# One slot table for both lots in the second expert layer, and one lookup for both choices

## The reference, cut to what matters

```python
x = x + _L0_attn_ref(_layernorm(x), ...)   # linear recurrence and a small MLP
x = x + _L0_ffn_ref(_layernorm(x), ...)    # 8 experts, 128 -> 256 -> 128, best 2 per row
x = x + _L1_attn_ref(_layernorm(x), ...)   # causal attention, 16 heads of 8
x = x + _L1_ffn_ref(_layernorm(x), ...)    # 8 experts, 128 -> 512 -> 128, best 2 per row
```

```python
scores = jax.nn.sigmoid(xf @ gate_w + bias)
top_scores, top_idx = jax.lax.top_k(scores, K)                  # K = 2 of E = 8
top_scores = top_scores / (jnp.sum(top_scores, axis=-1, keepdims=True) + 1e-06)
up = jnp.einsum('th,ehi->tei', xf, up_w) + up_b
eo = jnp.einsum('tei,eih->teh', gelu(up), down_w) + down_b      # only the 2 chosen are needed
combined = jnp.einsum('teh,te->th', eo * 0.1, w)
shared = (gelu(xf @ sw_up + sb_up) @ sw_down + sb_down) * 0.1
out = (shared + combined) / (max |shared + combined| per row + 1e-06)
```

## Time and profile before

| | |
|---|---|
| three executions | 942.72, 943.45, 945.0 us |
| the profiled execution, its own time | 942.91 us |
| its span (first to last instruction) | 941.1 us |
| PE busy | 792.7 us (84%), 5585 instructions |
| DVE busy | 603.0 us (64%) |
| ACT busy | 530.5 us (56%) |
| POOL busy | 425.1 us (45%) |
| mean granted TensorE clock | 0.925 of full |

### The profile page before, as it was taken

How to read it: one execution, slowest core, us unless ns; L and a number is a source line. 1 busy time by engine, 2 the same in 40 slices (tenths; PEclk the granted TensorE clock), 3 DMA queues, 4 the chain that set the end, 5 groups by cost and what they waited for, 6 DMA issues and landing times. The chain is left out here.

```text
span 941.1 us, 18633 instructions
## 1 busy us (share of the span) xinstructions
PE 792.7 (84%) x5585; PEld 596.8 (63%) x5585; DVE 603.0 (64%) x1378; ACT 530.5 (56%) x1108; POOL 425.1 (45%) x527
## 2 busy tenths in 40 slices
PE   2798833899749899999999999996648999999993
PEld 2566633898625556565655566554626999999773
DVE  5478744557649887777777777752650565678455
ACT  3466457566416566767677676674322656655541
POOL 2655467727468414232323332223367730372274
PEclk9999775999879999999999999997569999999997
DMA  5940013546253231313131312100012332342222
GB/s 142 367 125 1 17 48 95 176 124 164 70 176 124 65 99 37 101 33 100 34 105 41 105 53 82 34 1 1 9 42 78 113 105 59 98 115 64 80 70 64
DMA packets 82155, 80.45 MB, mean 85 GB/s; under 512 B 9856, under 2 KB 61758, under 8 KB 82110
## 3 DMA queue, kind: packets, MB, share of 16 engines
q1 hardware_dynamic: 73122, 62.68, 21.8%
q0 software_dynamic: 8192, 16.79, 6.1%
q10 hardware_dynamic: 796, 0.42, 0.2%
HBM read 41.06 MB, written 38.80 MB: 85 GB/s over the span
## 5 line engine op out<-in xcount | busy, mean ns | idle before, releaser
L1678 ACT ACTIVATE Pb<-ps,low 128x512 f32<-128x512 f32 x320 | 216.7, 689 | 131.4 <-PE ps L1777 87.5
L935 POOL DMA_INDIRECT YG<-yslots,slot x128 | 131.0, 1024 | 134.9 <-issue 69.9
L1556 DVE TENSOR_REDUCE m<-ps 128x4 f32<-128x1024 f32 x128 | 156.0, 1220 | 53.4 <-PE ps L1754 35.6
L1777 PE MATMUL ps<-Q,KZ 128*128 128x128 f32 (+3 forms) x512 | 172.1, 397 | 5.0 <-ACT Pb L1678 4.0
L392 POOL DMA_INDIRECT xslots<-XN,slot x128 | 125.7, 982 | 69.6 <-issue 37.6
L1487 POOL TENSOR_SCALAR_AFFINE_SELECT Pb<-Pb 128x512 f32<-128x512 f32 (+1 forms) x84 | 67.6, 805 | 190.1 <-ACT Pb L1678 189.4
L1777 PEld LDWEIGHTS ps<-Q,KZ 128*128 128x128 f32 x512 | 93.0, 192 | 81.8 <-ACT Pb L1678 56.1
L1341 PE MATMUL ps<-wdn,hb 128*128 128x128 f32 x960 | 133.9, 276 | 6.1 <-ACT hb L1160 5.7
L1163 ACT ACTIVATE hb<-ps,upb 128x128 f32<-128x128 f32 x320 | 91.4, 369 | 66.6 <-PE ps L1329 66.6
L1754 PE MATMUL ps<-KZ,Q 128*128 128x512 f32 x320 | 113.6, 433 | 13.9 <-DMA KZ<-terms 8.8
L1341 PEld LDWEIGHTS ps<-wdn,hb 128*128 128x128 f32 x960 | 120.1, 193 | 7.6 <-DVE yb L1193 6.9
(11 more groups left out here) (262 smaller groups left out, 1275.5 us busy)
## 6 DMA issues: line engine op xcount, KB each, us to landing
xt<-xslots SPq DMA_DIRECT2D x40, 256.0 KB
yslots<-yb SPq DMA_DIRECT2D x40, 256.0 KB, 2.3
terms<-high SPq DMA_DIRECT2D x32, 256.0 KB, 2.2
Q<-terms SPq DMA_DIRECT2D x128, 48.0 KB
KZ<-terms SPq DMA_DIRECT2D x128, 48.0 KB
xslots<-YG SPq DMA_DIRECT2D x2, 2560.0 KB, 11.8
terms<-low SPq DMA_DIRECT2D x16, 256.0 KB, 2.3
X<-in_L_attn_x_dram SPq DMA_DIRECT2D x4, 512.0 KB, 5.9
```

What stands on the lines that cost most here:

```text
L935: pool.indirect_dma_start(out=s.YG[:, TB * w + j, k, :], out_offset=None, in_=s.yslots[group][:, :], in_offset=bass.IndirectOffsetOnAxis(a ...
L1556: w = dve.tensor_reduce(top[:, :, (TB + 1, 3, TB, None, 1)[u]], ps.rearrange("p (t g k) -> p g t k", t=2, g=HG), AX.XY, ALU.max)
L1678: act.activation(Pb[:, NCH * (gg % 2) + c, :], bank(4 + c % 2), ACT.Exp, bias=s.low[:, :], scale=DH ** -0.5)\
L1777: w = pe.matmul(ps[:, col:col + T - kt * P], KZ[:, HG * gg + g, kt * P:kt * P + P], Q2[gg % 2][:, kt * P:T], start=True, stop=not masked)
```

## The change

In the second layer the two tables of 40 tiles become one of 72 (2 x 32 tiles of rows and 8 part tiles), so 9 bodies. The table is ordered by what the first lot fills: first the tiles that the first lot fills wholly, then the tiles that it begins and the second lot goes on with, then the tiles that only the second lot uses. At least 25 tiles are of the first sort, so the first 24 (`WHOLE`), three bodies, can be worked before the second lot is in; from body 3 on SP waits for the second lot's scatters. The first lot's rows lie in the first 40 tiles (`TOUCHED`), so its gathers wait for 5 bodies, as before. The first layer keeps its two lots of 40 tiles.

The second layer's places come from a new function, `place_phases`. In both functions the two choices are now looked up in one operation, the slots are announced (`placed`) before the tiles' expert numbers are worked out, and the matrix that counts rows before gives the count less one table (`before` filled with 0 and -1), so that one subtraction falls away. Both layers use one DRAM array for the table. The core of the diff:

```diff
-SLOTS = sum(GS)
-BODIES = SLOTS // (2 * TB)
+BT = 2 * TB
+WHOLE = (2 * TB * GROUPS[0] - (E - 1)) // BT * BT
+TOUCHED = -(-(2 * TB * GROUPS[0] + E - 1) // BT) * BT
+SLOTS = (sum(GS), -(-(2 * TB * B + E - 1) // BT) * BT)
+TILES = max(SLOTS)
...
@@ place (first layer)
     link(dve.tensor_tensor_scan(flatC, keep, inside, 0.0, ALU.mult, ALU.add))
-    link(dve.tensor_copy(tot, C[:, :, count - 1]))
-    link(dve.tensor_tensor(flatC, flatC, inside, ALU.subtract))
-    link(dve.tensor_tensor(flatC, flatC, before, ALU.add))
-    link(dve.tensor_scalar(toti, tot, float(P - 1), None, ALU.add))
+    link(dve.tensor_scalar(toti, C[:, :, count - 1], float(P - 1), None, ALU.add))
+    link(dve.tensor_tensor(flatC, flatC, behind, ALU.add))
...
+    hot = s.hot[:, :, tiles, :]
+    link(dve.tensor_tensor(hot, hot, place_of, ALU.mult))
+    link(dve.tensor_reduce(s.pos[:, :, tiles], hot, AX.X, ALU.add))
+    link(dve.tensor_scalar(s.slot[:, :, tiles], s.pos[:, :, tiles], 0.0, None, ALU.add))
+    dve.nop().then_inc(s.placed, 1)
...
-    for k in range(2):
-        hot, gt = s.hot[:, k, tiles, :], s.gt[:, tiles]
-        link(dve.tensor_tensor(hot, hot, pos, ALU.mult))
-        link(dve.tensor_reduce(gt, hot, AX.X, ALU.add))
-        if k == 0:
-            link(dve.tensor_copy(s.slot[:, k, tiles], gt))
-        else:
-            dve.tensor_copy(s.slot[:, k, tiles], gt).then_inc(s.placed, 1)
+    dve.nop().then_inc(s.numbered, 1)
...
+def place_phases(dve, s, link, g):
...
+    if g == 1:
+        heads = inside.rearrange("p (e j) -> p e j", e=E)[:, :, 0]
+        link(dve.tensor_tensor(heads, heads, s.count[:, :], ALU.add))
+    link(dve.tensor_tensor_scan(flatC, keep, inside, 0.0, ALU.mult, ALU.add))
+    total = C[:, :, count - 1]
+    if g == 0:
+        dve.tensor_copy(s.count[:, :], total)
+        dve.tensor_scalar(s.tilesi[:, 0, :], total, 0.0, None, ALU.add)
+    link(dve.tensor_scalar(s.tilesi[:, 1, :], total, float(P - 1), None, ALU.add))
+    link(dve.tensor_tensor(flatC, flatC, behind, ALU.add))
+    if g == 0:
+        link(dve.tensor_scalar(s.tilesi[:, :, :], s.tilesi[:, :, :], 7, None, ALU.arith_shift_right))
+        link(dve.tensor_copy(s.tiles[:, 0:4:3, :], s.tilesi[:, :, :]))
+        link(dve.tensor_tensor(part, begun, whole, ALU.subtract))
+        link(dve.tensor_tensor_scan(flat(s.tends, 0, 2), ones(2), flat(s.tiles, 0, 2), 0.0, ALU.mult, ALU.add))
+        link(dve.tensor_tensor(s.shifts[:, 0:2, :], s.tends[:, 0:2, :], s.tiles[:, 0:4:3, :], ALU.subtract))
+    else:
...
+    limit, low, step = (whole, begun)[g], s.shifts[:, g, :], s.step[:, g, :]
+    link(dve.tensor_tensor(step, s.shifts[:, g + 1, :], low, ALU.subtract))
+    link(dve.scalar_tensor_tensor(over, bc(limit), float(P), C, ALU.mult, ALU.is_le))
+    link(dve.tensor_tensor(over, over, bc(step), ALU.mult))
+    link(dve.tensor_tensor(over, over, bc(low), ALU.add))
+    link(dve.scalar_tensor_tensor(C, over, float(P), C, ALU.mult, ALU.add))
...
+    here, classes = slice((0, WHOLE)[g], (WHOLE, SLOTS[1])[g]), (1, 3)[g]
+    wide = [1, here.stop - here.start, classes * E]
...
+    link(dve.tensor_tensor(cmp, s.tileno[0:1, here].unsqueeze(2).broadcast_to(wide),
+                           flat(s.tends, 0, classes)[0:1, :].unsqueeze(1).broadcast_to(wide), ALU.is_ge))
+    link(dve.tensor_reduce(s.tef[0:1, here], cmp, AX.X, ALU.add))
...
@@ experts
+    BODIES = SLOTS[layer] // BT
+    SECOND, LAST = (SLOT0[1], WHOLE)[layer] // BT, [n // BT for n in (TOUCHED, SLOTS[layer])]
...
             rows_in(0)
-            for r in two:
-                load(0, 0, r)
-            for g in range(NG):
-
+            for n in range(2):
                 for r in two:
-                    load(g, 1, r)
-                    if g > 0:
-                        store(g - 1, GB[g - 1] - 1, r)
-                with sp.Fori(1, GB[g] - 1) as n:
+                    load(n, r)
+            for g, (start, end) in enumerate(((2, SECOND), (SECOND, BODIES))):
+                if g > 0:
+                    rows_in(g)
+                with sp.Fori(start, end) as n:
                     for r in two:
-                        load(g, n + 1, r)
-                        store(g, n - 1, r)
...
+                        load(n, r)
+                        store(n - 2, r)
...
-                    pool.wait_ge(stored[r], 16 * (BODY0[g] + GB[g]))
+                    pool.wait_ge(stored[r], 16 * LAST[g])
```

More of the change, by code:

```diff
@@ L118, in _ @@
             pool.wait_ge(cst, 8)
-            pool.affine_select(out=s.before[:, :], in_=s.before[:, :], compare_op=ALU.is_gt, fill=0.0, base=0,
+            pool.affine_select(out=s.before[:, :], in_=s.before[:, :], compare_op=ALU.is_gt, fill=-1.0, base=0,
                                pattern=[[1, P]], channel_multiplier=-1).then_inc(cst, 1)
@@ L346, in read_rank, with place @@
     dve.tensor_copy(s.rk[:, 0:2 * n], ps[:, 0:2 * n]).then_inc(s.rank_read, 1)
-def place(dve, s, link, g, layer=0):
-    dve.wait_ge(s.rank_read, NG * layer + g + 1)
+def place(dve, s, link, g):
+    dve.wait_ge(s.rank_read, g + 1)
     first, count = TB * FIRST[g], TB * GROUPS[g]
@@ new lines, in place_phases @@
+def place_phases(dve, s, link, g):
+    dve.wait_ge(s.rank_read, NG + g + 1)
+    first, count = TB * FIRST[g], TB * GROUPS[g]
+    tiles, n = slice(first, first + count), E * count
+    flatC, keep = s.C[:, E * first:E * first + n], s.keep[:, E * first:E * first + n]
+    C = flatC.rearrange("p (e j) -> p e j", e=E)
+    behind, inside = s.rk[:, 0:n], s.rk[:, n:2 * n]
+    wide = [P, E, count]
+    over = behind.rearrange("p (e j) -> p e j", e=E)
+    bc = lambda t: t.unsqueeze(2).broadcast_to(wide)
+    whole, part, new, begun, full = (s.tiles[:, k, :] for k in range(5))
+    flat = lambda t, a, b: t[:, a:b, :].rearrange("p k e -> p (k e)")
+    ones = lambda k: s.keep[:, E * NT:E * NT + k * E]
+    if g == 1:
[15 more added lines that the diff above has]
+    else:
+        link(dve.tensor_scalar(s.tilesi[:, 1, :], s.tilesi[:, 1, :], 7, None, ALU.arith_shift_right))
+        link(dve.tensor_copy(full, s.tilesi[:, 1, :]))
+        link(dve.tensor_tensor(new, full, begun, ALU.subtract))
+        link(dve.tensor_tensor_scan(flat(s.tends, 0, 3), ones(3), flat(s.tiles, 0, 3), 0.0, ALU.mult, ALU.add))
+        link(dve.tensor_tensor(s.shifts[:, 2, :], s.tends[:, 2, :], full, ALU.subtract))
+    limit, low, step = (whole, begun)[g], s.shifts[:, g, :], s.step[:, g, :]
[4 more added lines that the diff above has]
+    link(dve.scalar_tensor_tensor(C, over, float(P), C, ALU.mult, ALU.add))
+    place_of = C.rearrange("p e j -> p j e").unsqueeze(1).broadcast_to([P, 2, count, E])
+    hot = s.hot[:, :, tiles, :]
+    link(dve.tensor_tensor(hot, hot, place_of, ALU.mult))
+    link(dve.tensor_reduce(s.pos[:, :, tiles], hot, AX.X, ALU.add))
+    link(dve.tensor_scalar(s.slot[:, :, tiles], s.pos[:, :, tiles], 0.0, None, ALU.add))
+    dve.nop().then_inc(s.placed, 1)
+    here, classes = slice((0, WHOLE)[g], (WHOLE, SLOTS[1])[g]), (1, 3)[g]
+    wide = [1, here.stop - here.start, classes * E]
+    scratch = s.acc[0:1, :, :].rearrange("o j d -> o (j d)") if g == 0 else s.YG[0:1, :, :, :].rearrange("o j k d -> o (j k d)")
+    cmp = scratch[:, 0:wide[1] * wide[2]].rearrange("o (t u) -> o t u", u=wide[2])
+    link(dve.tensor_tensor(cmp, s.tileno[0:1, here].unsqueeze(2).broadcast_to(wide),
+                           flat(s.tends, 0, classes)[0:1, :].unsqueeze(1).broadcast_to(wide), ALU.is_ge))
+    link(dve.tensor_reduce(s.tef[0:1, here], cmp, AX.X, ALU.add))
+    if g == 0:
+        link(dve.tensor_scalar(s.te[0:1, here], s.tef[0:1, here], float(E - 1), None, ALU.min))
+    else:
+        link(dve.tensor_scalar(s.tei[0:1, here], s.tef[0:1, here], 0.0, None, ALU.add))
+        link(dve.tensor_scalar(s.te[0:1, here], s.tei[0:1, here], E - 1, None, ALU.bitwise_and))
+    dve.nop().then_inc(s.numbered, 1)
@@ L1033, in numbers @@
             s.te[0:1, bass.ds(first, count)], engines=[eng.engine], min_val=0, max_val=E - 1,
-            skip_runtime_bounds_check_because="place() writes min(count of ends, E - 1), which lies in 0 to E - 1")
+            skip_runtime_bounds_check_because="min(count of ends, E - 1) and count & (E - 1) lie in 0 to E - 1")
         return values
@@ L1210, in body @@
                 low = RING if layer else AHEAD
-                left = BT + UPS - low if not isinstance(i, int) else min(BT + UPS - low, SLOTS - BT * i - low)
+                left = BT + UPS - low if not isinstance(i, int) else min(BT + UPS - low, SLOTS[layer] - BT * i - low)
                 of_tile = numbers(dve, BT * i + low, left) if left > 0 else ()
@@ L1253, in _ @@
             body(0, True)
-            with dve.Fori(1, BODIES - LOOSE - 1) as i:
+            loose = BODIES - LOOSE - 1
+            with dve.Fori(1, loose) as i:
                 body(i, True)
-            for i in range(BODIES - LOOSE - 1, BODIES):
+            for i in range(loose, BODIES):
                 body(i, i < BODIES - 1)
```

(6 more changed lines are left out.)

89 lines of the change are left out of this document (41 added, 48 removed).

## The result

The changed kernel takes 928.36 us (median of four executions, 927.17 to 933.49), the kernel before 943.64 in the same comparison; the ratio is 0.9859, with a 95% interval of 0.9833 to 0.9886. The profiled execution took 928.71, its span is 927.0. The two spans, 941.1 and 927.0, differ by 14.1 us, and that difference can be followed place by place. In the second layer I measure from DVE's first operation of the routing stage (the reciprocal of the standard deviation, 652.39 before) to the first operation of the last combine (932.90 before): 280.5 us before.

The account below looks back on a forecast made before the run. PE was taken to set the pace in the bodies, with POOL's scatters and gathers at the ends. -15.17 + 2.8 + 1.2 - 2.15 = -13.3 gave 929.6 us profiled, 930.1 for the median, range 927 to 932.5 (0.78).

Parts of the forecast that it names:

- one body less: Second layer's bodies on PE: nine instead of ten, everything behind starts earlier, -15.17 us.
- places on DVE: Second layer's routing ahead of the boundary: DVE's new operations add 0.4 us (first lot) and 2.4 (second), taken as +2.8.
- wait ahead of body 3: PE waits for body 3's load, which follows the second lot's last scatter: +1.2 us, bounds 0.7 to 3.8.
- first combine: Second layer, now after body 5: its gathers arrive just in time, 0 us, up to +1.
- first layer: Slots announced earlier, so POOL's scatters and the boundary they set come sooner: -2.15 us, bounds 0 to -2.3.
- A: Rival: the wait ahead of body 3 is long enough to lower PE's clock, 2.6 plus 2.5 us, 935.2; chance 0.08.
- B: Rival: placing mis-sized; first layer's boundary stays (+2.15), DVE's new operations cost the upper bound (+2.2), 934.4; chance 0.07.
- C: Rival: DVE slows scatters beside the bodies, 48 us later, 977; decides from 0.42 us a scatter; chance 0.03.

Follow-up runs that it names:

- nine bodies alone: Kernel before with the second layer's tenth body left out (last 8 tiles not computed), tables, places and scatters as before: 928.16 us, ratio 0.9862.
- the run with POOL held: Changed kernel with eight clears of an unused buffer on POOL between the first and second lot's scatters in the second layer: 936.57 us, ratio 0.9941.
- slots announced last: Changed kernel with the second layer's slots announced after the tile numbers instead of before them: 927.12 us, ratio 0.9832.
- first layer's placing undone: Changed kernel with the first layer's place as before (tile numbers first, lookup per choice, slots last), except the dropped subtraction: 932.5 us, ratio 0.9893.
- the runs with early scatters: 14 instead of 10 scatters ahead of the second layer's boundary: changed kernel 924.55 us; also with second lot's numbers behind the boundary 924.42; kernel before 941.06.
- tile numbers later: Changed kernel with the second lot's tile numbers moved on DVE behind the boundary in front of the second expert stage: 927.43 us, ratio 0.9836.

## Why the prediction was right

The forecast was 930.1 us; 928.36 came. Term by term, in the profiled executions:

| term | forecast | measured | from |
|---|---|---|---|
| one body less | -15.17 | -15.17 | nine bodies alone |
| places on DVE | +2.8 | +3.0 | 6.18 - 5.85 and 8.76 - 6.06 |
| wait ahead of body 3 | +1.2 | +1.31, and 0.65 given back | PE's rows |
| first combine | 0 | 0 | no idle ahead of it |
| first layer | -2.15 | -2.47 at the boundary, -2.75 at the second layer | scatters at 131.75, reciprocal at 649.64 |

*The body.* Right, and shown by itself. PE was the bound, so its cost was read from the distance of two equal instructions rather than from a sum of durations.

*The places.* Right to 0.2 us. The estimated prices held: 1.35 for the compare over 1152 elements, 0.59 for the product whose second operand is read across. The 0.09 for an operation that waits for nothing is in none of the rows that the prediction names for it; the profile after bears it out (such operations start at 668.75, 668.84 and 668.91). What I had not counted is the small operation of 0.39, and each signal, put at 0.1, comes with 0.15 to 0.22 us of idle.

*The wait.* Its mechanism was right: the run with POOL held shows that it follows the last scatter one for one. That the size is right as well is in part luck. The boundary stands at nearly the same place in both profiles (694.49 and 694.71), so the forecast times can be held against the measured ones: SP's load went out at 765.60 (forecast 765.7), the transposes at 768.46 (768.7). But counted from the boundary both sides of the wait came sooner than forecast, the transposes after 73.75 us instead of 74.2, and PE was free for them after 72.4 instead of 73.0; in the difference the two errors nearly cancel. In two other runs with the same scatters and bodies the wait was 0.75 us (slots announced last) and 1.03 us (first layer's placing undone). The given-back part is the clock's: from the first transposes to those of body 3 it was 41.02 us before (with a body's distance added) and 41.68 after, 0.66 more in spite of 1.31 of wait, because PE's clock came back at 730 to 731 and not behind 731.5. The forecast has no term for this; it is chance, for in other runs of the changed bodies the clock came back later (last section).

*The first layer.* The mechanism was right and the size 0.3 low at the boundary: the scan began 0.18 earlier, ahead of anything in the places that was changed, and the rest of the places was a little faster. The further 0.28 at the start of the second layer lies within the spread of the last section. Undoing this part alone gave the 2.2 back at the boundary.

*The rivals.* A did not happen: the clock stayed at 1.00 behind 1.31 us of wait. Held to 6.59 us, PE lost 2.3 us by the clock, near the 2.5 that the rival has; a wait of the rival's own 3.8 us ahead of body 3 was not run. B: the first layer's boundary moved, and of the new operations only the one of 8 elements (0.39) came to more than double its price. C: the second lot's scatters are 1.30 us apart in the changed kernel, and 1.30 to 1.33 in the runs above; contention is there, 0.7 us for one scatter beside one compare, but far from 0.42 for each of 32.

The 1.7 us by which the median is faster than forecast are the sum of these small terms (0.9 in the profiled execution, 929.6 against 928.71); the rest lies within a spread of single executions of 6 us.

## What to carry to other kernels

Where one engine is busy without a gap, a unit of its work is worth the distance of two equal instructions, whatever else happens; check only that both ends of the stage move with it. When work is merged across a dependency, price the new wait by counting back from the last producer on its own engine (here 54 scatters in a row) and compare it with the time when the consumer gets there. And look at what a change leaves idle: POOL's wait ahead of the boundary had doubled, and four scatters moved into it gave a third of the change's own gain again.

## What the runs showed of the hardware

- A boundary that all engines cross does not open at the same distance from the last of them. Where DVE was last, POOL went on 1.6 us after DVE's last operation (its end at 693.14, POOL at 694.71 in the changed kernel); where POOL's scatters were last, 2.8 us after the last of these (rows of the runs with early scatters), and 2.96 and 2.97 at the first layer's boundary, before the change and after it (131.75 above). A scatter lands 2.23 us after its start, 1.27 after its issue of 0.96 ends; 1.27 and 1.6 make 2.8, as if the boundary waited for the landing. That is an estimate; no run tried it.

```profile
692.85 0.29 DVE L895 TENSOR_TENSOR gate<-wg 128x128 f32<-128x128 f32 x1
```

- The stretch ahead of the second layer's routing took 647.7 to 651.0 us in profiles of kernels whose code for it is the same, and 657.3 in one (tile numbers later), with the first bodies of the first layer starting within 2.5 us of each other. PE's mean granted clock was 0.918 in the span of that one and 0.925 to 0.930 in the others, but for the run with POOL held (0.920). In the slow one it was low in two places where the changed kernel's profile has 1.00: 0.86 from 275 to 300 and 0.80 from 325 to 350. Why it fell there was not tried; it is the spread against which all medians here are read.
- Behind a first wait of 2.91 to 3.9 us PE's clock was at half in each run, and it came back at no fixed place: before 731 for a start at 726.78 in the changed kernel, only in the course of 734 to 735 for a start at 728.25 in the run with the first layer's placing undone. That run needs 42.6 us to body 3, 1 us more than the changed kernel, though it waits 0.3 less there. A wait of that kind has no fixed price. Behind the waits of 0.75 to 2.13 us ahead of body 3 the clock stayed at 1.00; the 3.5 us that one expectation names is no limit that these runs show.
